# The halves of the second head added by GpSimd, in a new order of VectorE and TensorE, in an attention and feed-forward block

## The chip, the cores and the metric

The kernel runs on one core of a Trainium2 chip. The metric is the device time of one execution in microseconds (us); the median of several executions stands for a kernel.

## The reference

A batch of 64 sequences of 128 rows of width 256 passes a gated cross-attention and a gated feed-forward part. Only the first is touched here.

```python
qh, kh, vh = split_heads(layernorm(x) @ Wq), split_heads(ctx @ Wk), split_heads(ctx @ Wv)   # 16 heads of 64
dots = where(mask or causal, -max, qh @ kh.T * 64 ** -0.5)
x = x + tanh(g_xattn) * (merge_heads(softmax(dots) @ vh) @ Wo + bo)
x = x + tanh(g_ffn) * ffn(layernorm(x))            # quantised activations and weights
```

## The kernel before

Every engine has a program of its own, written out in order by hand, and they meet only at semaphores. The attention runs over 16 groups (`g`) of four sequences, and in each group over 8 steps (`c`) of two heads; `u = 8 g + c` numbers the 128 units. Each engine runs `step(g, c)` for all units through `drive`. `parts` says what a step holds: `new` is the projection of unit `u`, `soft` the softmax of unit `u - 1`, `old` the product with the values of unit `u - 3`; the product with Wo is that of unit `u - 4`.

A unit goes through the engines so. PE makes q and k in two PSUM banks used in turn (`proj`), and a quarter of the values for the group (`jobs` lists them; two banks, so each job waits until the job two places before it has been copied out). ACT copies q and k to SBUF. PE makes the scores of both heads. For each head VectorE (DVE) adds the mask (L635) and takes the maximum (L637), ACT takes four exponentials with their sums (L474), DVE scales the sums by 1/32768 and takes reciprocals (L623, L625), GpSimd (POOL) normalises the probabilities (L423), ACT makes their fp16 high part (L482), POOL the fp16 low part (L428), and a DMA issued by SP turns both parts (L362). DVE adds the two turned halves of each head (`join_prob`, L617), and PE multiplies them with the values (`times_v`, L882). ACT and DVE split that product into `o_hi` (L527) and `o_lo` (L674), which PE multiplies with Wo (`out_product`, L909).

The order in a step is, on PE: q, Wo product of `u - 4`, k, values, `times_v` of `u - 3`, scores of `u`. On DVE: both maxima of `u - 1`, both joins of `u - 3`, reciprocals of the first head, value copies (steps 0 to 2), reciprocals of the second head, then `o_lo` of `u - 3`, whose product is made in this same step, and last the work of the step: row statistics of the next group (step 1), moments (L580 to L588, step 2), statistics and moments of the second layernorm (step 4), its four normalisations (L748, step 5), the maximum (L753) and the four normalisations of the next group's rows (L602, step 6). The mask (step 0) and the residual (L735, step 3) stand earlier. In step 7 PE also turns the next group's rows and context (L853, four jobs `t`), ACT and DVE split each (L467, L610). POOL adds the bias to the residual's rows in step 5 (L439), and takes two powers a group (L415, L419).

The last group is followed by a drain, in which both joins are DVE's.

## Time and profile before

| | us |
|---|---|
| median of 3 runs | 1814.12 (1812.88 to 1816.78) |
| the profiled execution, its own time | 1819.5 |
| its span, first to last instruction | 1817.7 |
| PE, DVE, ACT, POOL busy | 1588.7, 1492.1, 1259.1, 778.9 |
| attention, first q copy to last masked scores | 16.6 to 1231 |
| mean granted TensorE clock | 0.968 |

Busy time is that of all instructions of an engine that overlap nothing of their own; matmuls are pipelined, so a row of one matmul is longer than the time until the next starts. The stages after the attention have the same code in both kernels.

### The profile page before, as it was taken

The page shows a single profiled execution, that of the slowest core. Times are in us where ns is not written, and L with a number is a line of the kernel's source. Part 1 is how long each engine was busy: PE and PEld are TensorE (multiplying, and loading weights), DVE is VectorE, ACT ScalarE, POOL GpSimd, SP SyncE. Part 2 cuts the span into 40 slices and gives each one's busy share as a digit, 9 for nine tenths or more (in the row PEclk, how much of TensorE's full clock was granted, in tenths as well). Part 3 has the DMA queues.
Part 4 walks back from the last instruction along what each step waited for, and adds up shares of the span by engine and source line. Part 5 has one row for each costly group of instructions (what it writes and reads, how often), then busy time and mean ns, then how long its engine had stood idle before and what let it go on. Part 6 is the DMA issues. An engine that isn't in the chain of part 4 may idle for free. (4 is left out here: it accounts for less than half of the span.)

```text
span 1817.7 us, 38253 instructions
## 1 busy us (share of the span) xinstructions
PE 1588.7 (87%) x12684; PEld 1285.3 (71%) x12684; DVE 1492.1 (82%) x2624; ACT 1259.1 (69%) x3238; POOL 778.9 (43%) x622
## 2 busy tenths in 40 slices
PE   7798888988889889898898988887998999895998
PEld 5676776767767677676676766666776777674887
DVE  6787878878788788787887878876888899898997
ACT  5576776766767666676666666665765899896665
POOL 3445545555455454454545545451000666560000
PEclk9899999999999999999999999989999899897999
DMA  5434434434344343344433533243996788474664
GB/s 168 110 83 106 88 88 92 102 86 92 82 92 105 88 98 82 81 107 92 92 82 81 117 82 92 54 87 113 341 327 224 264 279 302 149 289 174 196 208 150
DMA packets 351460, 252.22 MB, mean 139 GB/s; under 512 B 287792, under 2 KB 325808, under 8 KB 348464
## 3 DMA queue, kind: packets, MB, share of 16 engines
q1 hardware_dynamic: 351408, 251.58, 49.1%
q8 instruction: 26, 0.43, 0.1%
q14 instruction: 26, 0.21, 0.0%
HBM read 105.25 MB, written 76.02 MB: 100 GB/s over the span
## 5 line engine op out<-in xcount | busy, mean ns | idle before, releaser
L423 POOL TENSOR_TENSOR prob<-prob,rsums 128x512 f32<-128x512 f32 x256 | 265.5, 1040 | 560.1 <-DVE rsums L625 560.1
L474 ACT ACTIVATE prob<-masked,neg_max 128x128 f32<-128x128 f32 x1024 | 396.5, 389 | 154.5 <-DVE neg_max L637 153.2
L428 POOL TENSOR_TENSOR prob_parts<-prob,prob_parts 128x512 f16<-128x512 f32 x254 | 295.1, 1180 | 3.2 <-ACT prob_parts L482 1.5
L882 PE MATMUL pv<-probT,v_sb 128*64 128x128 f32 x2048 | 154.7, 283 | 112.3 <-DVE probT L617 89.6
L882 PEld LDWEIGHTS pv<-probT,v_sb 128*64 128x64 f32 x2048 | 111.2, 137 | 170.4 <-DVE probT L617 109.5
L482 ACT ACTIVATE prob_parts<-prob 128x512 f16<-128x512 f32 x254 | 160.1, 630 | 68.0 <-POOL prob L423 66.3
L674 DVE TENSOR_TENSOR o_lo<-pv,o_hi 128x512 fp32r<-128x512 f32 x125 | 86.4, 691 | 132.5 <-ACT o_hi L527 132.2
L474 ACT ACTIVATION_READ_ACCUMULATOR prob<-masked,neg_max 128x1 f32 x1024 | 192.6, 188 | 0.0
L637 DVE TENSOR_REDUCE neg_max<-masked 128x4 f32<-128x512 f32 x254 | 174.3, 686 | 8.8
L617 DVE TENSOR_TENSOR probT<-turn 128x512 f32<-128x512 f16 x254 | 172.4, 719 | 3.4 <-DVE mask_add L647 3.4
L635 DVE TENSOR_TENSOR masked<-score,mask_add 128x512 f32<-128x512 f32 x254 | 173.1, 682 | 1.6
L909 PE MATMUL y<-wo_hi,o_hi 128*128 128x256 f32 x508 | 151.5, 298 | 4.4 <-DVE o_lo L674 1.5
L501 ACT ACTIVATE qT<-proj 128x512 f32<-128x512 f32 x128 | 76.8, 600 | 101.1 <-PE proj L826 100.3
L909 PE MATMUL y<-wo_lo,o_hi 128*128 128x256 f32 x508 | 146.6, 289 | 0.0
L909 PE MATMUL y<-wo_hi,o_lo 128*128 128x256 f32 x508 | 146.5, 288 | 0.0
L2090 PE MATMUL y<-wd_both,h_hi 128*128 128x512 f32 x384 | 138.1, 404 | 4.8 <-ACT h_lo L1989 4.8
L1021 PE MATMUL pair<-xThi,wup_hi 128*128 128x512 f32 x312 | 125.2, 401 | 13.6 <-PEq L1381 5.8
L1660 POOL TENSOR_SCALAR xThi<-n_x 128x1024 fp32r<-128x1024 int16 x15 | 44.3, 2953 | 201.2 <-DMA n_x<-n_x_d 166.8
L896 PE MATMUL score<-kT,qT 64*64 64x128 f32 (+1 forms) x4096 | 119.2, 256 | 5.9 <-ACT kT L489 3.9
L1021 PE MATMUL pair<-xThi,wup_lo 128*128 128x512 f32 x312 | 123.7, 396 | 0.0
L1021 PE MATMUL pair<-xTlo,wup_hi 128*128 128x512 f32 x312 | 123.5, 396 | 0.0
L896 PEld LDWEIGHTS score<-kT,qT 64*64 64x64 f32 x4096 | 99.3, 137 | 29.2 <-issue 29.2
(252 smaller groups left out, 4404.0 us busy)
## 6 DMA issues: line engine op xcount, KB each, us to landing
gate<-gate_d SPq DMA_DIRECT2D x30, 768.0 KB, 4.3
n_x<-n_x_d SPq DMA_DIRECT2D x25, 512.0 KB, 5.0
gate_d<-stage SPq DMA_DIRECT2D x8, 1536.0 KB, 5.5
n_u_d<-w_raw SPq DMA_DIRECT2D x16, 768.0 KB, 4.0
stage<-n_u_d SPq DMA_DIRECT2D x16, 768.0 KB, 5.9
gate_d<-gate SPq DMA_DIRECT2D x7, 1536.0 KB, 5.5
x_in<-in_x SPq DMA_DIRECT2D x16, 512.0 KB, 4.2
ctx_in<-in_ctx SPq DMA_DIRECT2D x16, 512.0 KB, 5.1
```

What stands on the lines that cost most here:

```text
L423: gp.tensor_tensor(prob[:, h], prob[:, h], rsums[:, h, :].rearrange("p (b o) -> p b o", o=1).broadcast_to([P, NB, P]), ALU.mult).then_inc( ...
L428: gp.tensor_tensor(prob_parts[:, h, 1], prob[:, h].rearrange("p b k -> p (b k)"), prob_parts[:, h, 0], ALU.subtract).then_inc(prob_low, 1)
L474: nc.scalar.activation(prob[:, h, b, :], masked[:, h, b, :], ACT.Exp, bias=neg_max[:, h, b:b + 1], accum_out=psums[:, h, b:b + 1]).then_in ...
L482: nc.scalar.activation(prob_parts[:, h, 0], prob[:, h].rearrange("p b k -> p (b k)"), ACT.Copy).then_inc(prob_high, 1)
L617: nc.vector.tensor_tensor(probT[:, h], turn[:, slot, h, 0:NB], turn[:, slot, h, NB:2 * NB], ALU.add).then_inc(probT_copied[h], 1)
L635: nc.vector.tensor_tensor(masked[:, h], score[h][:], mask_add[:], ALU.add).then_inc(masked_done, 1)
L637: nc.vector.tensor_reduce(neg_max[:, h, :], masked[:, h], X, ALU.max, negate=True).then_inc(max_done, 1)
L882: last = nc.tensor.matmul(pv[h * HD:(h + 1) * HD, b, :], v_sb[:, b, c * P + h * HD:c * P + (h + 1) * HD], probT[:, h, b, :], start=True, s ...
L896: last = nc.tensor.matmul(score[h][half * HALF:(half + 1) * HALF, b, 0:keys], qT[rows[h], at:at + HALF], kT[rows[h], b * P:b * P + keys], ...
L909: last = nc.tensor.matmul(y[:, e, :], o[s][:, e * P:(e + 1) * P], w[m][:, c * D:(c + 1) * D], start=(c == 0 and j == 0 and e % 2 == 0), st ...
L1021: last = nc.tensor.matmul(bank, stat(s, k), mov(m, k), start=(j == 0), stop=(j == len(passes) - 1))
L2090: nc.tensor.matmul(y[b][:, e], h_hi[:, h, cols], wd[:, :, at:at + D], start=(h == 0 and j == 0), stop=(h == 1 and j == HJ - 1), skip_group ...
```

## The change

The adding of the second head's turned halves moves from DVE to POOL (`join_second`), where it stands first in the step. The scaling of the sums moves from DVE to POOL too, as a product of reciprocal and constant on 128x4 elements before each normalising. On DVE a step now runs: maximum of the first head, `o_lo` of `u - 4` (one step later than before), join of the first head, maximum of the second head, reciprocals, a first part of the step's own work, reciprocals of the second head, value copies, and the rest of that work. PE makes k before the Wo product and not behind it; in step 7 the turnings stand elsewhere. ACT copies k between the exponentials of the two heads in every step. POOL's bias addition moves from step 5 to 6.

```diff
     for c in range(NC):
-        jobs += [(c, "q", 0)]
-        if c == NC - 1:
-            jobs += [(c, "t", n) for n in range(KC)]
-        jobs += [(c, "k", 0)]
+        jobs += [(c, "q", 0), (c, "k", 0)]
         jobs += [(c, "v", n) for n in V_AT[c]]
-    jobs += [(NC - 1, "t", n) for n in range(KC, 2 * KC)]
+    jobs += [(NC - 1, "t", n) for n in range(2 * KC)]
...
             def normalise_prob(u, h):
                 gp.wait_ge(recip_done, 2 * u + h + 1)
-                gp.tensor_tensor(prob[:, h], prob[:, h], rsums[:, h, :].rearrange("p (b o) -> p b o", o=1).broadcast_to([P, NB, P]),
+                gp.tensor_tensor(scaled[:, h], rsums[:, h], pscale[:], ALU.mult).then_inc(sum_scaled, 1)
+                gp.wait_ge(sum_scaled, 2 * u + h + 1)
+                gp.tensor_tensor(prob[:, h], prob[:, h], scaled[:, h, :].rearrange("p (b o) -> p b o", o=1).broadcast_to([P, NB, P]),
                                  ALU.mult).then_inc(normed, 1)
...
+            def join_second(u, slot, times):
+                gp.wait_ge(prob_turned[1][slot], 16 * times)
+                wait(gp, pv_done, u)
+                gp.tensor_tensor(probT[:, 1], turn[:, slot, 1, 0:NB], turn[:, slot, 1, NB:2 * NB],
+                                 ALU.add).then_inc(probT_copied[1], 1)
             def step(g, c):
                 u, new, soft, old, more = parts(g, c)
+                if old:
+                    join_second(u - 3, (c + 1) % 2, NC // 2 * g + (c - 1) // 2)
                 if c == 3 and new and more:
                     make_rstd(g + 1)
                 if c == 5 and new:
                     if not (isinstance(g, int) and g == 0):
                         make_rstd2(g - 1)
+                if c == 6 and new:
                     gp.wait_ge(xres_loaded, 16 * (g + 1))
                     gp.tensor_tensor(xres[:], xres[:], bo_g[:].rearrange("p (o n) -> p o n", o=1).broadcast_to([P, NB, D]),
                                      ALU.add).then_inc(xres_ready, 1)
...
-                if nxt:
-                    for i, n in ts[:KC]:
-                        high(g, i, n)
                 if soft:
                     exps(u - 1, 0)
-                if new and k_first:
+                if nxt:
+                    high(g, *ts[0])
+                if new:
                     copy_k(g, c, u)
                 if nxt:
-                    high(g, *ts[KC])
+                    high(g, *ts[1])
                 if soft:
                     exps(u - 1, 1)
-                if new and not k_first:
-                    copy_k(g, c, u)
                 if nxt:
-                    high(g, *ts[KC + 1])
+                    high(g, *ts[2])
...
+                if nxt:
+                    high(g, *ts[3])
...
             def reciprocals(u, h):
                 dve.wait_ge(exp_done, NB * (2 * u + h + 1))
                 wait(dve, normed, 2 * u + h - 1)
-                nc.vector.tensor_scalar(psums[:, h, :], psums[:, h, :], 1.0 / PSCALE, None, ALU.mult).then_inc(sum_scaled, 1)
-                dve.wait_ge(sum_scaled, 2 * u + h + 1)
                 nc.vector.reciprocal(rsums[:, h, :], psums[:, h, :]).then_inc(recip_done, 1)
+            def maxima(u, h):
+                n = 2 * u + h + 1
+                dve.wait_ge(scored, n)
+                wait(dve, exp_done, NB * (n - 2))
+                nc.vector.tensor_tensor(masked[:, h], score[h][:], mask_add[:], ALU.add).then_inc(masked_done, 1)
+                dve.wait_ge(masked_done, n)
+                nc.vector.tensor_reduce(neg_max[:, h, :], masked[:, h], X, ALU.max, negate=True).then_inc(max_done, 1)
+            def attended_low(u):
+                dve.wait_ge(out_high, u + 1)
+                wait(dve, wo_done, u)
+                nc.vector.tensor_tensor(o_lo[:], hand.banks[1][:], o_hi[:].bitcast(F32), ALU.subtract).then_inc(out_split, 1)
...
                 if soft:
-                    for h in range(2):
...
-                        if nxt:
-                            low(g, *jobs_of(c, "t")[h], 2 * KC * (g + 1) + h)
-                if c == 0 and new:
...
+                    maxima(u - 1, 0)
+                if oldest:
+                    attended_low(u - 4)
                 if old:
-                    for h in range(2):
-                        join_prob(u - 3, h, (c + 1) % 2, NC // 2 * g + (c - 1) // 2)
+                    join_prob(u - 3, 0, (c + 1) % 2, NC // 2 * g + (c - 1) // 2)
                 if soft:
+                    maxima(u - 1, 1)
                     reciprocals(u - 1, 0)
-                if new and c < 3:
...
+                if c == 0:
+                    make_mask(g)
+                if c == 1 and more:
+                    layernorm_stats(g + 1)
+                if c == 2 and more:
+                    layernorm_moments(g + 1)
+                if c == 3 and after_first:
+                    residual(g)
+                if c == 4 and after_first:
+                    second_stats(g - 1)
+                if c == 5 and after_first:
+                    second_norm(g - 1, 0, NB // 2)
+                if c == 6 and after_first and more:
+                    second_max(g - 1)
                 if nxt:
-                    low(g, *jobs_of(c, "t")[KC], 2 * KC * (g + 1) + KC)
+                    for n in range(2):
+                        low(g, *ts[n], 2 * KC * (g + 1) + n)
                 if soft:
                     reciprocals(u - 1, 1)
-                if c == 3 and not (isinstance(g, int) and g == 0):
-                    residual(g)
+                if c < 3:
+                    values(g, c)
+                if c == 4 and after_first:
+                    second_moments(g - 1)
+                if c == 5 and after_first:
+                    second_norm(g - 1, NB // 2, NB)
+                if c == 6 and more:
+                    normalise(g + 1)
                 if nxt:
-                    low(g, *jobs_of(c, "t")[KC + 1], 2 * KC * (g + 1) + KC + 1)
-                if old:
...
-                    nc.vector.tensor_tensor(o_lo[:], hand.banks[1][:], o_hi[:].bitcast(F32), ALU.subtract).then_inc(out_split, 1)
+                    for n in range(2, 4):
+                        low(g, *ts[n], 2 * KC * (g + 1) + n)
...
                         work(n)
-                after_first = new and not (isinstance(g, int) and g == 0)
-                if c == 1 and new and more:
...
-                if c == 6 and new and more:
-                    normalise(g + 1)
...
+            def second_moments(g):
                 moments(stats2, mean2, vare2, stats2_done, MOMENTS * g + NB, var2_ready)
...
-            def second_norm(g):
+            def second_norm(g, first, end):
                 dve.wait_ge(rstd2_ready, g + 1)
                 wait(dve, xn2_stored, 16 * g)
-                for b in range(NB):
+                for b in range(first, end):
                     nc.vector.tensor_scalar(xn2[:, b, :], x1[:, b, :], mean2[:, b:b + 1], rstd2[:, b:b + 1],
...
+            maxima(U - 1, 0)
+            attended_low(U - 4)
             for h in range(2):
                 join_prob(U - 3, h, 1, U // 2 - 1)
+            maxima(U - 1, 1)
             reciprocals(U - 1, 0)
             reciprocals(U - 1, 1)
             attended_low(U - 3)
...
                 src = (x_in, ctx_in)[n // KC]
                 for e in range(NB):
+                    if then is not None and e == NB - 1:
+                        scores_free(*then)
                     last = nc.tensor.transpose(proj[b][:, e * P:(e + 1) * P], src[:, e, (n % KC) * P:(n % KC + 1) * P], ident[:])
                 last.then_inc(projected[b], 1)
...
+                if first or second:
+                    pe.wait_ge(w_ready, 2 if first else 5)
+                if new:
+                    weights_left(g, c, jobs_of(c, "k")[0][0], 1)
                 if nxt:
                     transpose_in(g, *ts[0])
                 if oldest:
...
                     out_product(u - 4, (c - 4) % NC)
                 if nxt:
                     transpose_in(g, *ts[1])
-                if first or second:
-                    pe.wait_ge(w_ready, 2 if first else 5)
-                if new:
-                    weights_left(g, c, jobs_of(c, "k")[0][0], 1)
-                if nxt:
-                    transpose_in(g, *ts[2])
                 if first or fourth:
                     pe.wait_ge(w_ready, 3 if first else 6)
                 if new:
                     for i, n in jobs_of(c, "v"):
                         value(g, i, n)
                 if nxt:
-                    transpose_in(g, *ts[3])
+                    transpose_in(g, *ts[2])
                 if old:
-                    times_v(u - 3, co, (g, c, u) if new else None)
+                    times_v(u - 3, co, (g, c, u) if new and not nxt else None)
+                if nxt:
+                    transpose_in(g, *ts[3], (g, c, u))
                 if new:
-                    if not old:
+                    if not (nxt or old):
                         scores_free(g, c, u)
                     scores(g, c, u)
```

## Rows read from the trace of the kernel before

**Rows 1.** Timeline of ACT, the q copies of step 0 of groups 1 and 15.

```profile
98.17 0.60 ACT L501 ACTIVATE qT<-proj 128x512 f32<-128x512 f32 x1
...
1148.79 0.60 ACT L501 ACTIVATE qT<-proj 128x512 f32<-128x512 f32 x1
```

**Rows 2.** Windows, steps 0 to 7 of group 9, from q copy to q copy; columns: window, length, then busy of each engine.

```profile
698.52:707.90 9.38, 9.37 (x87) 7.83 (x88) 8.15 (x17) 6.22 (x21) 5.05 (x6) 1.00 0.63 168
707.90:715.49 7.59, 7.59 (x80) 6.31 (x80) 5.77 (x15) 6.02 (x22) 4.34 (x5) 1.00 0.39 78
715.49:723.89 8.40, 7.88 (x80) 6.32 (x80) 7.24 (x16) 6.03 (x21) 4.56 (x5) 1.00 0.33 62
723.89:733.56 9.67, 7.89 (x81) 6.33 (x80) 8.90 (x20) 6.39 (x22) 5.44 (x6) 1.00 0.28 54
733.56:741.15 7.59, 7.59 (x80) 6.31 (x80) 5.52 (x13) 6.40 (x22) 4.32 (x5) 1.00 0.79 207
741.15:751.21 10.06, 7.83 (x78) 5.96 (x77) 7.35 (x22) 6.39 (x23) 7.32 (x7) 1.00 0.27 52
751.21:761.43 10.22, 8.04 (x78) 6.16 (x78) 8.12 (x16) 6.38 (x22) 4.58 (x5) 1.00 0.40 103
761.43:774.35 12.92, 10.19 (x88) 8.34 (x88) 9.75 (x21) 7.94 (x25) 3.42 (x4) 0.87 0.21 41
```

**Rows 3.** Timeline of PE, step 1 of group 9: first matmuls of q, Wo product, k, and the rest.

```profile
706.12 0.50 PE L826 MATMUL proj<-tx_hi,wq_hi 128*128 128x512 f32 x1
...
707.61 0.28 PE L909 MATMUL y<-wo_hi,o_hi 128*128 128x256 f32 x1
...
709.02 0.40 PE L826 MATMUL proj<-tc_hi,wk_hi 128*128 128x512 f32 x1
...
711.86 1.09 PE L882 MATMUL pv<-probT,v_sb 128*64 128x128 f32 x16
...
713.71 0.50 PE L826 MATMUL proj<-tx_hi,wq_hi 128*128 128x512 f32 x1
```

**Rows 4.** Waits, 400 to 1200 us: engine, line, releaser, total, times, longest.

```profile
PE pv L882 <- DVE probT L617: 55.2, 31, 3.1
```

**Rows 5.** Timeline of DVE, end of step 4 and start of step 5 of group 9.

```profile
740.43 1.39 DVE L741 BATCH_NORM_STATS2 stats<-x 128x6 f32<-128x256 f32 x4
...
742.77 0.69 DVE L635 TENSOR_TENSOR masked<-score,mask_add 128x512 f32<-128x512 f32 x1
...
745.42 1.87 DVE L617 TENSOR_TENSOR probT<-turn 128x512 f32<-128x512 f16 x2
```

**Rows 6.** Timeline of ACT, step 1 of group 9: q copy, k copy behind eight exponentials.

```profile
707.90 0.60 ACT L501 ACTIVATE qT<-proj 128x512 f32<-128x512 f32 x1 [0.76 <-PE proj L826]
...
711.48 0.57 ACT L489 ACTIVATE kT<-proj 128x512 f32<-128x512 f32 x1
```

**Rows 7.** Timeline of DVE: both joins in step 1, then one sum of the moments in step 2.

```profile
709.36 1.28 DVE L617 TENSOR_TENSOR probT<-turn 128x512 f32<-128x512 f16 x2
...
723.38 1.14 DVE L582 TENSOR_TENSOR v_sum<-stats 128x4 f32<-128x4 f32 x1
```

**Rows 8.** Timeline of POOL, beside the moments of step 2 and the joins of step 5.

```profile
722.19 2.31 POOL L428 TENSOR_TENSOR prob_parts<-prob,prob_parts 128x512 f16<-128x512 f32 x2
...
743.77 2.37 POOL L439 TENSOR_TENSOR xres<-xres,bo_g 128x1024 f32<-128x1024 f32 x1
```

**Rows 9.** Groups of POOL by line, whole span: busy, mean ns, idle before.

```profile
L423 POOL TENSOR_TENSOR prob<-prob,rsums 128x512 f32<-128x512 f32 x256 | 265.5, 1040 | 560.1 <-DVE rsums L625 560.1
...
L415 POOL TENSOR_TENSOR rstd<-vare,mhalf 128x4 f32<-128x4 f32 x16 | 16.3, 1020 | 16.2 <-DVE vare L588 16.2
...
L450 POOL TENSOR_SCALAR tg_small<-tg 128x1 f32<-128x1 f32 x1 | 0.2, 225 | 0.0
```

**Rows 10.** Groups of DVE by line, 400 to 1200 us.

```profile
L623 DVE TENSOR_SCALAR psums<-psums 128x4 f32<-128x4 f32 x170 | 49.4, 291 | 24.4 <-ACT prob L474 24.4
...
L748 DVE TENSOR_SCALAR xn<-x,mean,rstd 128x256 f32<-128x256 f32 x40 | 22.4, 617 | 0.0
```

More of the change, by code:

```diff
@@ L627, in step, with values @@
+            def values(g, c):
+                for i, n in jobs_of(c, "v"):
+                    b, before = nth(g, i)
+                    dve.wait_ge(projected[b], before + 1)
+                    nc.vector.tensor_copy(v_sb[:, n % NB, 0:VH], proj[b][:]).then_inc(copied[b], 1)
             def step(g, c):
                 u, new, soft, old, more = parts(g, c)
+                oldest = not isinstance(g, int) or u >= 4
                 nxt = c == NC - 1 and new and more
+                ts = jobs_of(c, "t")
+                after_first = not (isinstance(g, int) and g == 0)
@@ L767, in _ @@
             drive(dve, step)
-            def attended_low(u):
-                dve.wait_ge(out_high, u + 1)
-                dve.wait_ge(wo_done, u)
-                nc.vector.tensor_tensor(o_lo[:], hand.banks[1][:], o_hi[:].bitcast(F32), ALU.subtract).then_inc(out_split, 1)
             def ffn_low_part(n):
```

63 lines of the change are left out of this document (18 added, 45 removed).

## Prediction

> **What bounds the kernel now.** I read the page first, for the share of each engine, and then only the attention, since the later stages have the same code. The q copies give its beat: from group 1 to group 15 there are 14 groups in 1148.79 - 98.17 us, 75.04 each [rows 1]. Cut at the q copies, the windows show where a group's time lies: steps 1 and 4 take 7.59, the others up to 12.9 [rows 2]. In the two short steps PE is busy without a gap, so 7.59 is PE's own time for a step, and the timeline of one shows its parts: q 1.49, Wo product 1.41, k and values 2.84 together, values' product and scores 1.85 [rows 3]. Step 0 has a second quarter of the values (1.42 more, 9.0). Step 7 has none, but four turnings: four f32 matmuls of 128 columns each; the 16 of the values' product, which run in pairs, take 1.09, so one turning is about 0.52, and the step 7.59 - 1.42 + 2.1 = 8.3. A group in which PE never waits would take 9.0 + 6 x 7.59 + 8.3 = 62.8. It takes 12.2 more.
>
> What PE waits for is the join: 31 waits of 55.2 us in total between 400 and 1200 us [rows 4]. The timeline of DVE around step 5 shows why. The own work of step 4 (statistics from 740.43) stands ahead of the maxima of the next step, which begin at 742.77, and the two joins follow at 745.42 [rows 5]. DVE's cycle is thus: values' product ends, ACT makes `o_hi`, DVE makes `o_lo`, its own work, both maxima (2.65), both joins, and only then PE may multiply again. A step with much own work lengthens PE's step by what is over PE's slack. DVE is not full: 60.8 of 75.8 in this group [rows 2]. POOL is busy 39.0 of them.
>
> **The change part by part.** (1) DVE loses one join a step, 1.28 / 2 = 0.64 [rows 7], and two scalings, 0.29 each [rows 10]: 1.2 x 8 = 9.8 a group. It is left with 51 of PE's 62.8. (2) The order: I follow one step from the start of q, at 0. Scores are there at about 0.2. DVE: first maximum to 1.5, `o_lo` (as long as one mask addition, 0.66) to 2.2, join to 2.85, second maximum to 4.2, reciprocals, first own part from 4.4. ACT copies q at 1.8 [rows 3, 6] and, since eight exponentials take 3.09 less the copy's 0.5, say 1.55 a head, has the first head done at 3.8, k copied at 4.4, the second head done at 5.95. The second reciprocals come at 6.1. PE wants `o_lo` at 1.49 + 1.41 = 2.9, the joins and k at about 5.75, and is through at 7.59. So in a bare step nothing waits, and own work of 1.7 us between the two reciprocals lies beside the exponentials, where it costs nothing; with no such cover it would cost what it costs now. That takes away the 12.2 but for what follows. The wait for the k copy at the values' product goes too, because k is made 1.41 sooner and copied before the second head.
>
> What is late next? `o_lo` is now made in the very step that uses it, with 0.7 us of slack. Whatever DVE still does when the scores are there, beyond that, stops PE. Behind the second reciprocals, at 6.3, there are 1.5 us left to the next scores: enough for values, not always for moments (step 4) and four normalisations (step 6).
>
> (3) The price of POOL. Its join is not in the trace; a product over the same 128x512 takes 1.04 [rows 9] and the low parts 2.31 for two [rows 8]; I take 1.17. Its scaling on 128x4 is bounded by 0.23 (a small one-input instruction) and 1.02 (a power on 128x4) [rows 9]. A power is not a product, so I take 0.3 with its wait. A step costs POOL 1.17 + 2 x 0.3 + 2 x 1.04 + 2.31 = 6.2, and a group with two powers and the bias addition (2.37 [rows 8]) 49.6 + 4.4 = 54, under 62.8. The order within POOL is good: its second low part ends about 2.2 us into the next step, the join to 3.4, and PE wants it at 5.75. SP's queue keeps its order; the turning of a head has three steps until its join, against a landing of a few microseconds, so I cost it at nothing; the low parts and the next high part are half a step apart.
>
> (4) Collisions. Two DVE instructions show that a POOL instruction can hold them up: the 128x4 sum at 723.38 took 1.14 [rows 7], to the end of the second low part, which ran from about 723.35 to 724.50 [rows 8]; and the joins at 745.42 took 1.87 and not 1.28 [rows 5, 7], while the bias addition ran until 746.14 [rows 8]. The scaling's mean of 0.29 and 0.617 for 256 columns of the second normalisations [rows 10] fit: instructions that read two things from SBUF wait. Additions with a PSUM input, as the maxima's, show none. The Trainium skill, SBUF — State Buffer, section "SBUF: two separate sides", says the same: one shared pair, an exclusive lock for the whole instruction. By that rule the collisions are whole POOL instructions and not a shared pace, and the trace agrees (the sum ends with the low part, to 0.02 us).
>
> POOL is now busy nearly without a break from the second reciprocals (6.2) to 3.4 in the next step. So the parts that DVE does behind the second reciprocals run into it. Step 4: seven small instructions, of which two or three are held for 1.04 to 1.17: they end 2.2 late, less 0.7 of slack, 1.6 us of wait (between 0 and 2.7). Step 5: two normalisations there, 0.3 (0 to 1.5). Step 6: four of them, and the bias addition has just pushed POOL back; they end 1.6 to 5.2 into step 7, which needs them for its first turning and `o_lo`; with the serial chain of turnings, copies and low parts in step 7 I take 2.5 (1.2 to 4.8). Step 7 itself: the fourth low part waits for ACT, which has four more copies than usual, and ends about 1.5 into step 0: 0.8. The other five steps together 0.3. The sum is 5.5 of the 12.2 back: a group of 68.3, or 6.8 less than now, 14 x 6.8 = 95. In groups 0 and 15, which have loads and weight work of their own, I take 5 each, as the same order holds but DVE has more own work (nothing to 10 each). The drain keeps its instructions. Together 105.
>
> The same skill, GPSIMD Engine Reference, section "Engine selection", speaks against moving an addition: elementwise work belongs on VectorE, where two-input work is about twice as fast. The rows agree, 0.64 against 1.04 to 1.17. It would make the join dearer by 0.5 a unit, which would tell only if POOL were the bound.
>
> The sum is made against the profiled execution: 1819.5, of which the span is 1817.7 and 1.8 lies around it. It gives 1714.5. That execution is 5.4 above the median of the runs, 1814.12, more than their highest; I apply the same saving to the median: 1709.
>
> **Rivals.** A: the collisions are nearly harmless (the lower ends: 0, 0, 1.2, 0.5). A group of 64.5, 147 saved, with 12 for groups 0 and 15: 1655. For it: DVE has 51 us of work, and a short instruction may slip in between two of POOL. B: they are at their upper ends (2.7, 1.5, 4.8, with 1 each for step 7 and the rest): 73.8 and 17 saved, 1790; halfway between it and mine 71, 57 + 5 saved, 1752. For it: POOL's chain of product, two low parts and join is 4.4 us without a gap, and it is the very stretch in which DVE's late parts stand; step 7's stop also fell with the clock, 0.87 in its window [rows 2], which a longer stop brings back. C, the other side: POOL becomes the bound. If the 128x4 product costs 1.02 as the power does, with 0.1 for its wait, a step is 7.8, a group 62 + 4.4, plus the joins that hold it (8 x 0.64) and six more held instructions of 0.35 and moments, some 4: 76, or 1 x 14 slower, 1828. It decides from about 1.0 us for that product on; below 0.6 POOL has slack again. Against it: 0.23 for the other small instruction. D: no change within 0.2%, because the beat is set by something that I don't see, 1814; the two steps at exactly 7.59 with PE full speak against it.
>
> **How the numbers follow.** Mine (1680 to 1740) 0.5; A 0.17; B with its half way 0.23; D 0.03; C 0.07. The predicted time is 1709. Faster by over 0.2% (3.6 us, about what a measurement of this kernel can tell from no change) are mine, A and nearly all of B: 0.89; same 0.03, slower 0.08. The range for 8 in 10 leaves out half of A's lower side and the upper end of B with C: 1655 to 1775.
>
> **What the profile after would show.** Right: q copies 68 apart a group; steps 0 to 3 within 0.3 of PE's own time; no wait of the values' product for a join of DVE, but waits of the Wo product for `o_lo` and of the first turning for DVE in steps 5 and 7; POOL's 128x4 product near 0.2 and its join near 1.17; POOL busy about 140 + 60 us more; single small DVE instructions of about 1 us ending with one of POOL. Wrong: waits for POOL's join at the values' product (C); steps 5 and 7 at 7.6 and 8.3 (A); waits of ACT for a turned part before the high parts, which I cost at nothing.

## The result, and the profile after

The changed kernel takes 1677.05 us (median of 4 runs, 1674.65 to 1681.05) against 1815.45 (1812.88 to 1817.66) for the kernel before in the same session: a ratio of 0.924 (95% interval 0.9217 to 0.9264), 138 us less. The forecast was 1709 in a range of 1655 to 1775. The profiled execution took 1674.65, its span is 1672.8, which is 144.9 less than the 1817.7 of before.

Each engine's busy time over the span, from the page of the changed kernel:

```profile
PE 1558.6 (93%) x12684; PEld 1270.2 (76%) x12684; DVE 1376.2 (82%) x2243; ACT 1254.1 (75%) x3238; POOL 1022.8 (61%) x1004
```

DVE has 116 us less work than before (1492.1), POOL 244 more (778.9), while PE and ACT have the same work. The mean granted clock is 0.977 (0.968). The timeline of ACT gives the beat of the groups, again from the q copies of groups 1 and 15, beside [rows 1]:

```profile
92.91 0.60 ACT L509 ACTIVATE qT<-proj 128x512 f32<-128x512 f32 x1 [0.56 <-PE proj L840]
...
1012.55 0.60 ACT L509 ACTIVATE qT<-proj 128x512 f32<-128x512 f32 x1 [0.47 <-PE proj L840]
```

That is 65.69 a group where it was 75.04: 14 x 9.35 = 131 of the 145 us. Group 0 takes 76.7 and not 81.6, group 15 to its last q copy 67.2 and not 72.9, another 10.6. Some 3 us lie elsewhere. The windows of group 9, steps 0 to 7, beside [rows 2]:

```profile
618.47:628.13 9.66, 9.38 (x86) 7.45 (x86) 7.38 (x15) 6.11 (x21) 6.91 (x9) 1.00 0.62 165
628.13:635.75 7.62, 7.62 (x80) 6.33 (x79) 6.59 (x14) 5.99 (x21) 4.94 (x7) 1.00 0.37 74
...
651.00:658.62 7.62, 7.62 (x80) 6.33 (x79) 7.06 (x19) 6.37 (x22) 6.43 (x8) 1.00 0.79 206
658.62:666.56 7.94, 7.89 (x80) 6.25 (x79) 6.42 (x14) 6.57 (x22) 6.80 (x8) 1.00 0.34 66
666.56:675.16 8.60, 8.38 (x82) 6.64 (x81) 8.01 (x14) 6.28 (x22) 8.44 (x9) 1.00 0.47 122
675.16:684.16 9.00, 8.07 (x87) 6.45 (x86) 5.59 (x11) 7.71 (x27) 6.94 (x9) 1.00 0.30 58
```

Steps 1 to 4 (2 and 3 are left out, 7.62 and 7.63) are PE's own time, with PE busy throughout. What is left over it is 0.32 in step 5, 0.98 in step 6, and about 0.7 each in steps 0 and 7, where PE's own time, 9.0 and 8.3, is the prediction's reckoning and not a measurement. Step 7 was 12.92 and at a clock of 0.87; it is 9.00 at full clock.

The waits of the changed kernel, 400 to 1000 us (engine, line, releaser; total, times, longest):

```profile
PEld y L925 <- DVE o_lo L643: 10.7, 18, 0.7
...
PEld proj L840 <- DVE tc_lo L617: 8.5, 18, 0.7
...
PE proj L869 <- ACT kT L498: 3.6, 9, 0.4
...
PE proj L840 <- ACT v_sb L528: 2.1, 9, 0.3
```

The wait of the values' product for a join, 55.2 us in [rows 4], is gone. What remains of PE's waits is short. In PE's own rows it is 4.7 us for the low parts of the turned rows and 2.6 for `o_lo`, both DVE's, and 5.7 for ACT's copies of k and of the values. None is put down to the join that POOL now makes. The two groups of POOL that are new, over the whole span (busy, mean ns, idle before):

```profile
L434 POOL TENSOR_TENSOR probT<-turn 128x512 f32<-128x512 f16 x125 | 177.7, 1421 | 0.0
L420 POOL TENSOR_TENSOR scaled<-rsums,pscale 128x4 f32<-128x4 f32 x256 | 58.8, 230 | 181.7 <-DVE rsums L630 181.4
```

The small product costs 0.23, and the join 1.42 where 1.17 was taken.

The step with the most over PE's own time is step 6. This is its end in group 9, POOL first, then DVE, then ACT:

```profile
669.28 2.38 POOL L448 TENSOR_TENSOR xres<-xres,bo_g 128x1024 f32<-128x1024 f32 x1
```

```profile
671.42 2.08 DVE L609 TENSOR_SCALAR x_in<-x_in,mean,rstd 128x256 f32<-128x256 f32 x4
```

```profile
673.15 0.63 ACT L491 ACTIVATE prob_parts<-prob 128x512 f16<-128x512 f32 x1 [1.85 <-POOL prob L422]
...
675.16 0.60 ACT L509 ACTIVATE qT<-proj 128x512 f32<-128x512 f32 x1
```

The bias addition makes POOL's first product late (it ends at 673.03). ACT waits 1.85 for it, and the copy of the values and that of q stand behind it in ACT's order. PE's k then waits 0.22 for the value copy (at 674.32). The q copy that ends this window is late too, so part of the 0.98 is PE's only in step 7: from q's first matmul to the next, the two steps take 7.64 and 9.95 (664.80, 672.44, 682.39). PE waits 0.41 there for ACT's copy of k (at 678.31) and 0.52 for the low part of the third turning (at 682.39). Between 400 and 1000 us it never waits for `x_in`, although the four normalisations take 2.08.

Now the collisions. DVE at the end of step 4 of group 9:

```profile
655.19 0.18 DVE L630 RECIPROCAL rsums<-psums 128x4 f32<-128x4 f32 x1 [0.42 <-ACT prob L483]
655.30 0.17 DVE L587 TENSOR_TENSOR m_sum<-stats 128x4 f32<-128x4 f32 x1
...
655.73 0.16 DVE L592 TENSOR_TENSOR m_sq<-m_dif 128x4 f32<-128x4 f32 x1
655.80 1.03 DVE L593 TENSOR_SCALAR v_eps<-v_sum 128x4 f32<-128x4 f32 x1
656.86 1.09 DVE L595 SCALAR_TENSOR_TENSOR vare<-m_sq,v_eps 128x4 f32<-128x4 f32 x1
```

and POOL beside it:

```profile
651.41 1.69 POOL L434 TENSOR_TENSOR probT<-turn 128x512 f32<-128x512 f16 x1
...
655.45 0.23 POOL L420 TENSOR_TENSOR scaled<-rsums,pscale 128x4 f32<-128x4 f32 x1 [0.57 <-DVE rsums L630]
655.76 1.04 POOL L422 TENSOR_TENSOR prob<-prob,scaled 128x512 f32<-128x512 f32 x1
656.76 2.29 POOL L427 TENSOR_TENSOR prob_parts<-prob,prob_parts 128x512 f16<-128x512 f32 x2
```

Of seven instructions on 128x4, five take 0.16 and two take 1.03 and 1.09. `v_eps` starts with POOL's product and ends as that ends (655.80 + 1.03 = 656.83, against 656.76 to 656.80). `vare` is let in there and ends with the first low part. The other five start from 655.30 to 655.73, before POOL's product (655.76): a window of some 0.4 us behind the reciprocals, open because POOL first makes its own small product.

### The profile page after: what moved, and what is told of

Its sections match the earlier page's. It is cut to its first block and busy times, and to the rows that moved or that the text cites. A ratio compares the mean times of both kernels' runs of the same rounds, so it can differ in the third digit from the quotient of the medians.

```text
span 1672.8 us, 38339 instructions
## 1 busy us (share of the span) xinstructions
PE 1558.6 (93%) x12684; PEld 1270.2 (76%) x12684; DVE 1376.2 (82%) x2243; ACT 1254.1 (75%) x3238; POOL 1022.8 (61%) x1004
## 5 line engine op out<-in xcount | busy, mean ns | idle before, releaser
L427 POOL TENSOR_TENSOR prob_parts<-prob,prob_parts 128x512 f16<-128x512 f32 x254 | 299.3, 1197 | 4.2 <-ACT prob_parts L491 2.4
L422 POOL TENSOR_TENSOR prob<-prob,scaled 128x512 f32<-128x512 f32 x256 | 269.8, 1054 | 20.0
L434 POOL TENSOR_TENSOR probT<-turn 128x512 f32<-128x512 f16 x125 | 177.7, 1421 | 0.0
L420 POOL TENSOR_TENSOR scaled<-rsums,pscale 128x4 f32<-128x4 f32 x256 | 58.8, 230 | 181.7 <-DVE rsums L630 181.4
L898 PE MATMUL pv<-probT,v_sb 128*64 128x128 f32 x2048 | 141.6, 281 | 3.7 <-DVE probT L624 2.8
L925 PE MATMUL y<-wo_lo,o_hi 128*128 128x256 f32 x508 | 144.9, 285 | 0.0
L2106 PE MATMUL y<-wd_both,h_hi 128*128 128x512 f32 x384 | 134.6, 394 | 4.7 <-ACT h_lo L2005 4.7
L925 PEld LDWEIGHTS y<-wo_hi,o_hi 128*128 128x128 f32 x508 | 97.3, 191 | 37.4 <-DVE o_lo L643 34.4
L624 DVE TENSOR_TENSOR probT<-turn 128x512 f32<-128x512 f16 x129 | 123.4, 958 | 0.0
```

The costliest lines, as they stand in the source:

```text
L422: gp.tensor_tensor(prob[:, h], prob[:, h], scaled[:, h, :].rearrange("p (b o) -> p b o", o=1).broadcast_to([P, NB, P]), ALU.mult).then_inc ...
L427: gp.tensor_tensor(prob_parts[:, h, 1], prob[:, h].rearrange("p b k -> p (b k)"), prob_parts[:, h, 0], ALU.subtract).then_inc(prob_low, 1)
L434: gp.tensor_tensor(probT[:, 1], turn[:, slot, 1, 0:NB], turn[:, slot, 1, NB:2 * NB], ALU.add).then_inc(probT_copied[1], 1)
L624: nc.vector.tensor_tensor(probT[:, h], turn[:, slot, h, 0:NB], turn[:, slot, h, NB:2 * NB], ALU.add).then_inc(probT_copied[h], 1)
L898: last = nc.tensor.matmul(pv[h * HD:(h + 1) * HD, b, :], v_sb[:, b, c * P + h * HD:c * P + (h + 1) * HD], probT[:, h, b, :], start=True, s ...
L925: last = nc.tensor.matmul(y[:, e, :], o[s][:, e * P:(e + 1) * P], w[m][:, c * D:(c + 1) * D], start=(c == 0 and j == 0 and e % 2 == 0), st ...
```

## The experiments

Times are medians and the ratios are to the kernel before in the same session, with the 95% interval. "Group" is the mean of the 14 groups, read as above from the q copies. An edit is against the changed kernel unless it says otherwise.

**Both joins on DVE again, in the new order.**

```diff
-                if old:
-                    join_second(u - 3, (c + 1) % 2, NC // 2 * g + (c - 1) // 2)
...
                 if old:
-                    join_prob(u - 3, 0, (c + 1) % 2, NC // 2 * g + (c - 1) // 2)
+                    for h in range(2):
+                        join_prob(u - 3, h, (c + 1) % 2, NC // 2 * g + (c - 1) // 2)
```

> The changed kernel with both joins back on VectorE, one behind the other, and everything else as changed: the new order without the second head's offload. My theory (VectorE is not full; what paid is that its own work and the low part no longer stand between two products with the values): the second join delays the second maximum, and so the second exponentials, by 0.6 us, of which the step has most in hand; a group goes from 65.7 to some 66.3, the kernel to about 1686. Rival (the offloaded join is a real part of the gain): each step is longer by about the join's 0.64 us, a group 70.8, the kernel about 1755.

Measured: 1752.33, 0.966 (0.9644 to 0.9676), a group of 70.75. The steps of group 9 are 9.57, 7.62, 7.62, 7.66, 7.90, 9.19, 10.18, 11.29. In size that is the rival's, but not in its manner: steps 0 to 3 have not grown, so a second join has room on DVE in a bare step. All of it is in steps 4 to 7, and the timeline of DVE in this kernel shows how, at the end of step 6:

```profile
713.26 4.49 DVE L622 TENSOR_TENSOR probT<-turn 128x512 f32<-128x512 f16 x2
```

with POOL beside it:

```profile
714.36 2.84 POOL L446 TENSOR_TENSOR xres<-xres,bo_g 128x1024 f32<-128x1024 f32 x1
```

Two joins of 0.64 each take 4.49. The pair starts beside the low parts and ends 0.55 behind the bias addition (717.20), about the length of one join. So a part of what the joins on DVE cost is time in which POOL holds them; a later run shows how much goes with the bias addition. My figure had left that out.

**The moved work alone, in the order of before.** The second join and the scaling go to POOL as in the change; all else is the kernel before, against which the diff stands. It shows the join alone; the scaling's lines are those of the change.

```diff
                 if old:
-                    for h in range(2):
-                        join_prob(u - 3, h, (c + 1) % 2, NC // 2 * g + (c - 1) // 2)
+                    join_prob(u - 3, 0, (c + 1) % 2, NC // 2 * g + (c - 1) // 2)
...
+                if old:
+                    join_second(u - 3, (c + 1) % 2, NC // 2 * g + (c - 1) // 2)
```

> The kernel before, in its old order, with the second head's join and the scalings of both heads moved to GpSimd: the offload without the order. My theory: VectorE's cycle from one product with the values to the next is shorter by 0.64 us in the five or six steps that are bound by it, a group 71.5, the kernel about 1765. Rival (the offload is what pays): most of the 138 us, about 1690 to 1710. Other rival (in the old order GpSimd's join comes too late or collides): no gain, 1815.

Measured: 1846.0, 1.0181 (1.0163 to 1.0199), a group of 76.79. The sign was wrong. The waits of this kernel, 400 to 1200 us:

```profile
PE pv L893 <- DVE probT L631: 39.9, 30, 2.9
PE pv L893 <- ACT kT L503: 34.3, 40, 1.2
```

The wait for DVE's join fell only from 55.2 [rows 4] to 39.9, and that for k's copy rose (14.5 before). And what DVE does on its own became slower, here the moments of step 2, DVE and then POOL:

```profile
740.67 1.14 DVE L596 TENSOR_TENSOR v_sum<-stats 128x4 f32<-128x4 f32 x1
741.85 1.09 DVE L598 TENSOR_SCALAR mean<-m_sum 128x4 f32<-128x4 f32 x1
```

```profile
739.49 2.29 POOL L433 TENSOR_TENSOR prob_parts<-prob,prob_parts 128x512 f16<-128x512 f32 x2
741.75 1.16 POOL L440 TENSOR_TENSOR probT<-turn 128x512 f32<-128x512 f16 x1
```

POOL's join stands right behind the low parts, and so holds the next of DVE's instructions: `mean` averages 631 ns between 400 and 1200 us where it was 170, a normalisation of `xn` 862 (617, [rows 10]), one of `x_in` 647 (406), all over the same stretch.

**The moved work alone, with k copied between the exponentials in every step.** This takes away the wait for k and asks whether it was the cause. The diff is against the last kernel.

```diff
-                k_first = c in (0, NC - 1)
+                k_first = True
```

> The kernel before in its old order, with join and scalings moved to GpSimd as in the run before on this (1846), and ACT's copy of k between the two heads' exponentials in every step. In that run the product with the values waited less for the join (39.9 against 55.2 us in 800) but more for k's copy (34.3 against 14.5). Theory: the wait for k, which stands behind both maxima and all exponentials, took up what the shorter join gave: with k copied early the gain comes out, a group 73 to 74.5, the kernel about 1795. Rival (the loss is GpSimd's join holding up VectorE's own work, and k only fills in): about 1835 to 1846.

Measured: 1871.36, 1.0306 (1.0281 to 1.0331), a group of 78.55. The wait for k is gone, and the time is still 25 us more:

```profile
PE pv L893 <- DVE probT L631: 61.3, 31, 2.8
...
PE proj L864 <- DVE x_in L616: 44.6, 11, 4.1
```

The wait for k had only filled in ahead of that for DVE. The copy in its new place also makes the second head's sums later: DVE waits 84.5 us for exponentials where it waited 64.5. My expectation fell. The rival had the loss stay with k copied early, but it gave 1835 to 1846, and no run here separates what POOL's join holds up from the rest of the 31 us.

**The Wo product ahead of k again.**

```diff
+                if oldest:
...
+                    out_product(u - 4, (c - 4) % NC)
...
                 if new:
                     weights_left(g, c, jobs_of(c, "k")[0][0], 1)
...
-                if oldest:
...
-                    out_product(u - 4, (c - 4) % NC)
```

> The changed kernel with PE's Wo product again ahead of k, VectorE's new order kept. By my step table PE then wants the low part at 1.5 us of a step, and VectorE has it at 2.25: 0.7 us of wait in all 8 steps, not given back, so a group of 71.5 and the kernel about 1770. Rival (the low part is ready earlier than I worked out, or the delay is absorbed): 1677 to 1685.

Measured: 1895.89, 1.0454 (1.0435 to 1.0472), a group of 79.54. Every bare step has about the wait that the reckoning in the prediction gives (0.7 of slack less 1.41), as PE's timeline shows:

```profile
767.39 0.39 PE L925 MATMUL y<-wo_hi,o_hi 128*128 128x256 f32 x1 [0.64 <-DVE o_lo L643]
```

Steps 1 to 4 take 8.52 to 8.58, 0.9 more, together 3.6 of the 12.7 that group 9 has grown by (the row ahead of a wait is longer than PE's pace, so a row's wait is less than what the step grows by). The rest is in steps 5, 7 and 0 (10.01, 14.62, 11.03), where PE waits 2.13, 2.70 and 1.76 for `o_lo`. That fits a slack of nothing, at which whatever makes DVE late goes to PE in full. I had counted the first part only.

**All own work of DVE behind the second reciprocals and value copies.**

```diff
                 if c < 3:
                     values(g, c)
+                if c == 0:
+                    make_mask(g)
+                if c == 1 and more:
+                    layernorm_stats(g + 1)
...
```

> The changed kernel with all own work of VectorE's step (mask, statistics, moments of the first layernorm, residual, first two normalisations, maximum) behind the second reciprocals and the value copies, none between the two reciprocals. My theory: the stretch between the reciprocals is free time beside the exponentials, and behind them only 1.5 us are left and GpSimd is in the way: waits of PE for the low part in steps 2, 4, 5 and 6, a group of about 70, the kernel about 1740. Rival (VectorE has slack enough, the place doesn't matter): 1677 to 1685.

Measured: 1870.9, 1.0309 (1.0292 to 1.0326), a group of 79.1. The direction was right; the size is three times what I gave, 194 us and not 63. The worst is step 3 with 13.26. Ahead of it, DVE has the moments of step 2 beside POOL's whole chain:

```profile
751.86 0.89 DVE L587 TENSOR_TENSOR m_sum<-stats 128x4 f32<-128x4 f32 x1
752.67 0.15 DVE L588 TENSOR_TENSOR m_dif<-stats 128x4 f32<-128x4 f32 x1
752.74 1.14 DVE L589 TENSOR_TENSOR v_sum<-stats 128x4 f32<-128x4 f32 x1
753.91 1.08 DVE L591 TENSOR_SCALAR mean<-m_sum 128x4 f32<-128x4 f32 x1
...
754.98 1.12 DVE L593 TENSOR_SCALAR v_eps<-v_sum 128x4 f32<-128x4 f32 x1
```

Seven instructions on 128x4, 0.86 us when nothing holds them (below), take 4.4. PE then waits 3.85 for `o_lo` (at 758.42). The mean clock is 0.947.

**The bias addition in step 7, between POOL's two products.**

```diff
-                if c == 6 and new:
-                    gp.wait_ge(xres_loaded, 16 * (g + 1))
...
                         normalise_prob(u - 1, h)
+                        if h == 0 and c == 7 and new:
+                            gp.wait_ge(xres_loaded, 16 * (g + 1))
...
```

> The changed kernel with GpSimd's bias addition (2.4 us) moved from step 6, ahead of both products, to step 7, between the two. My theory: the 1.0 us that step 6 and the 0.5 us that step 7 take over PE's own time come from the addition, which makes the first product, ACT's high part and the value copy behind it late; a group goes from 65.7 to some 64.4, the kernel to about 1658. Rival (VectorE's four normalisations are what is late): 1677, as they stay where they are. Other rival (in step 7 it makes the second product late and comes back in step 0): 1677 or more.

Measured: 1686.76, 0.9289 (0.9273 to 0.9305), a group of 66.18, 0.5 more than the changed kernel. Step 6 fell to 7.63 as forecast, but step 7 rose to 10.01 and step 5 to 8.46. The four normalisations at the end of step 6, in this kernel:

```profile
675.74 2.92 DVE L609 TENSOR_SCALAR x_in<-x_in,mean,rstd 128x256 f32<-128x256 f32 x4
```

They took 2.08 in the changed kernel (671.42 to 673.50). There the bias addition had pushed POOL back, and its first product ended at 673.03, with 0.3 until the second. Now the product (676.26 to 677.34) is followed by two low parts without a gap. In step 7 PE now waits 0.42 for `o_lo`, which it did not in the changed kernel. So the addition was what made step 6 long, as in my theory, but moving it made a collision elsewhere. Step 5's 0.5 more goes with a wait of 0.57 for `o_lo`; why it grew was not followed up.

**Normalisations between the reciprocals in step 6, the maximum behind them,** on top of the last edit. The maximum reads one tensor and nothing else.

```diff
-                if c == 6 and after_first and more:
-                    second_max(g - 1)
+                if c == 6 and more:
+                    normalise(g + 1)
...
-                if c == 6 and more:
-                    normalise(g + 1)
+                if c == 6 and after_first and more:
+                    second_max(g - 1)
```

> The changed kernel with the bias addition in step 7, as in the run before, and in step 6 the four normalisations between the reciprocals and the maximum (which reads one SBUF operand) behind them. With the addition alone moved, step 6 lost its 1.0 us, but the normalisations met the second product and the low parts, took 2.9 us and not 2.1, and step 7 was 1.0 longer. My theory: between the reciprocals they meet one product at most, and the maximum behind them is not held: a group of 65.0, the kernel about 1668. Rival (the four are held as long there, and the second reciprocals come late instead): 1680 or more.

Measured: 1664.78, 0.9164 (0.9148 to 0.918), a group of 65.02. Step 7 is 9.01 again and step 6 stays at 7.63. The maximum, now beside POOL's chain, takes 1.18 us in all ten groups between 400 and 1000 us, and it took 1.19 in the changed kernel, inside the bias addition (669.61 to 670.80): POOL doesn't hold it.

**The moments of step 4 between the reciprocals too,** on top of that.

```diff
                 if c == 4 and after_first:
                     second_stats(g - 1)
+                    second_moments(g - 1)
...
-                if c == 4 and after_first:
-                    second_moments(g - 1)
```

> The kernel of the run with the bias addition in step 7 and the normalisations of step 6 between the reciprocals (1665), and in step 4 the seven moments' instructions ahead of the second reciprocals instead of behind them. Behind them the last two are held by GpSimd's second product and first low part, about 1 us each, and step 5 is 8.25 and not 7.62. My theory: ahead of them GpSimd's first product is over and nothing holds them; the second reciprocals are 0.7 us late, which GpSimd makes good in the next step; step 5 at 7.65 to 7.8, a group of 64.5, the kernel about 1657. Rival (the late reciprocals only move the whole chain and step 5 meets it with the second product for the values): 1665 or more.

Measured: 1657.21 (1655.95 to 1658.63), 0.9129 (0.9116 to 0.9141), a group of 64.44. The moments of step 4 run ahead of the second reciprocals, all seven at their own length; of these the first and last:

```profile
641.97 0.17 DVE L587 TENSOR_TENSOR m_sum<-stats 128x4 f32<-128x4 f32 x1
...
642.67 0.16 DVE L595 SCALAR_TENSOR_TENSOR vare<-m_sq,v_eps 128x4 f32<-128x4 f32 x1
```

POOL is between its two products there (none from 642.04 to 643.10). The moments of step 2 stand between the reciprocals as well, and there `vare` is still held by the first product, 0.88 at 626.34, at no cost: steps 1 to 6 are now 7.62 or 7.63. This kernel beats both: 1.2% less than the changed one (0.9129 / 0.924). In group 9 PE has two waits left, 0.28 for `o_lo` in step 0 (at 607.29) and 0.33 for the low part of the third turning (at 668.28).

**In step 7, the third high part of the turned rows ahead of the second exponentials.**

```diff
                 if nxt:
                     high(g, *ts[1])
-                if soft:
-                    exps(u - 1, 1)
                 if nxt:
                     high(g, *ts[2])
                 if soft:
+                    exps(u - 1, 1)
+                if soft:
                     high_prob(u - 1, 0, c % 2, NC // 2 * g + c // 2)
```

> The changed kernel with ACT's copy of the third turning (step 7) ahead of the second head's exponentials. My theory: the 0.5 us that q waits in step 0 for the low part of that turning go, and nothing else becomes late: a group 65.2, the kernel about 1669. Rival (the exponentials, the second product and the low parts are 0.5 us later, and the wait for the Wo product's low part in step 0 grows by as much): 1677.

Measured: 1680.09, 0.925 (0.9233 to 0.9267), a group of 65.91: no gain. The wait that should have gone is still there: the q of step 0 waits 0.63 where it waited 0.52.

**POOL's join made twice,** the first time into a tile that nobody reads; this is added work, and nothing is left out.

```diff
+                gp.tensor_tensor(spare[:], turn[:, slot, 1, 0:NB], turn[:, slot, 1, NB:2 * NB], ALU.add)
                 gp.tensor_tensor(probT[:, 1], turn[:, slot, 1, 0:NB], turn[:, slot, 1, NB:2 * NB],
                                  ALU.add).then_inc(probT_copied[1], 1)
```

> The changed kernel with GpSimd's addition of the halves made twice in every step, first into a spare tile: GpSimd has 1.2 us more a step. My theory: GpSimd is not the bound, in steps 0 to 2 and 4 the second addition fits ahead of the first product, and only steps 3, 5, 6 and 7, which have the powers and the bias addition, get longer: a group 67 to 69, the kernel about 1710. Rival (GpSimd with 54 us a group is as good as the bound): 8 x 1.2 = 9.4 a group, the kernel about 1825.

Measured: 1726.45, 0.9514 (0.9486 to 0.9541), a group of 68.88; steps 9.66, 7.62, 7.63, 8.39, 7.91, 8.49, 10.20, 9.00. In steps 0 to 2 another 1.2 us on POOL costs nothing, so POOL is not the bound there. It costs in steps 3 to 6, which have powers, the bias addition or late parts of DVE: 3.2 a group for 8 x 1.2 of work. In step 6 PE waits 1.36 for ACT's copy of the values (0.22 in the changed kernel), as the first product is later still.

**Both joins on DVE, and the bias addition in step 7.** This tests whether the first experiment's loss comes from the joins being held by the bias addition.

The edit is that of the bias addition, on top of the first experiment (the lines taken out of step 6 are left out):

```diff
                         normalise_prob(u - 1, h)
+                        if h == 0 and c == 7 and new:
+                            gp.wait_ge(xres_loaded, 16 * (g + 1))
...
```

> Both joins on VectorE, as in the run before on this, and the bias addition in step 7. There the joins of step 6 took 4.5 us instead of 1.3, held to the end of the bias addition. Theory of the collisions (what the offload saves is not the join's 0.64 us but that VectorE stands behind GpSimd's chains): step 6 and 7 lose most of their surplus of 3.9 us over the changed kernel, a group 68.5, the kernel about 1715. Rival (it is VectorE's load): 1750, unchanged.

Measured: 1717.76, 0.9464 (0.9442 to 0.9486), a group of 68.29. Of the 75 us that the joins on DVE cost, 35 go with the place of one POOL instruction, though in the changed kernel the same move costs 9 (0.9289 against 0.924). Step 6 falls from 10.18 to 7.98. The other 40 stay. They are in steps 5 (9.19 as before) and 7 (10.87) above all, where PE waits 1.63 and 1.19 for `o_lo`. A second join of 0.64 makes DVE that much later in the step, and its last two moments are held for 1.03 and 1.09 as in the changed kernel; how much of the 40 is length and how much is holding was not separated.

**The scaling back on DVE, the join on POOL.**

```diff
-                gp.tensor_tensor(scaled[:, h], rsums[:, h], pscale[:], ALU.mult).then_inc(sum_scaled, 1)
-                gp.wait_ge(sum_scaled, 2 * u + h + 1)
...
+                nc.vector.tensor_scalar(psums[:, h, :], psums[:, h, :], 1.0 / PSCALE, None, ALU.mult).then_inc(sum_scaled, 1)
+                dve.wait_ge(sum_scaled, 2 * u + h + 1)
                 nc.vector.reciprocal(rsums[:, h, :], psums[:, h, :]).then_inc(recip_done, 1)
```

> The changed kernel with the scaling of the sums back on VectorE, ahead of the reciprocals; the join stays on GpSimd. My theory: 0.16 us of VectorE for 0.28 us of GpSimd's chain, both with room in most steps, so 1670 to 1685, no difference beyond 0.5%. Rival (VectorE's scalings are held behind GpSimd's product, as some were in the kernel before, 0.7 us each): a group 67 or more, the kernel about 1700.

Measured: 1748.69, 0.9639 (0.9618 to 0.9661), a group of 70.5. About half a microsecond a step on DVE, in a kernel whose bare steps have room for it, costs 72 us. The end of step 4, DVE:

```profile
697.16 0.18 DVE L630 RECIPROCAL rsums<-psums 128x4 f32<-128x4 f32 x1
...
697.62 0.90 DVE L589 TENSOR_SCALAR mean<-m_sum 128x4 f32<-128x4 f32 x1
...
698.51 1.14 DVE L591 TENSOR_SCALAR v_eps<-v_sum 128x4 f32<-128x4 f32 x1
699.68 1.08 DVE L593 SCALAR_TENSOR_TENSOR vare<-m_sq,v_eps 128x4 f32<-128x4 f32 x1
```

and POOL:

```profile
697.42 1.07 POOL L420 TENSOR_TENSOR prob<-prob,rsums 128x512 f32<-128x512 f32 x1 [0.77 <-DVE rsums L630]
```

POOL's product now starts 0.26 after the start of the reciprocals and not 0.57, and three moments are held, not two. It is the same with the normalisations: `x_in` averages 1004 ns against 579, `xn` 737. (Means over 400 to 1200 us; `xn` took 401 in the changed kernel.) So the small product on POOL bought a window. It is not the only thing that it bought, for the scaling itself is held as well, once in every group, to the end of the bias addition, DVE and then POOL:

```profile
713.68 1.05 DVE L628 TENSOR_SCALAR psums<-psums 128x4 f32<-128x4 f32 x1
```

```profile
711.86 2.84 POOL L446 TENSOR_TENSOR xres<-xres,bo_g 128x1024 f32<-128x1024 f32 x1
```

In 9 of 16 groups this takes 2.17, in 7 it takes 1.05; the mean over all scalings, 265 ns, hides it. PE waits for `o_lo` 1.95 in step 5 and 1.19 in step 7 of group 9. The 72 us were not divided between the two.

## Why the prediction was right, and where its sizes were off

**The bound and the order: right.** The own work of DVE in front of the joins was what PE waited for: put behind the second reciprocals it costs 194 us. The order with the scaling on POOL, but not the join, gives 62 of the 138 us (first experiment), and bare steps run at PE's own 7.62. The slack of 0.7 at `o_lo` was worked out well: take away the 1.41 of the Wo product and PE waits 0.64 in each bare step. The copy of k at the values' product went as forecast.

**The fall of DVE's load (9.8 a group): too large, and wrong as a reason.** In group 9 DVE's busy time fell from 60.8 to 53.4, that is by 7.4, as instructions that POOL holds count as busy (the first join now averages 0.96 and not 0.72). Join and scaling on POOL in the old order made the kernel 31 us slower, while in the new order the join's move is worth 75 and the scaling's 72. Their worth is not simply in what DVE no longer does, as bare steps take either on DVE without a loss. The parts need each other.

**POOL's prices: nearly right.** The small product 0.23 and not 0.3, the join 1.42 and not 1.17. Alone it takes 1.17; the rest is its wait for DVE's join, which reads SBUF at the same time (1.69 at 651.41). The lock holds in both directions, which the forecast did not price. POOL was busy 54.5 of group 9, forecast 54. Rival C fell with the 0.23, and the doubled join shows room left in the bare steps.

**Collisions: the mechanism right, the size too large, and one path missed.** This is the step that was off: 5.5 a group was taken, 2.9 is measured over PE's 62.8. Moments and second normalisations together: 0.3 and not 1.9, because two moments are held but the other five pass ahead of POOL's product, and the slack takes up most of the two. For the four normalisations of step 6 and the chain behind them 2.5 was taken. They took 2.08, held by one product of POOL, the next mask addition follows at 673.43, and PE waits neither for `x_in` nor, in step 7, for `o_lo`. What steps 6 and 7 have over PE's time, 1.0 + 0.7, came in good part by a path that the forecast had no term for. The bias addition delays POOL's first product, ACT waits for that, and from 673.15 to its copy of k at 677.67 it has no gap left, so that its copies of the values and of k are late for PE. The run with the addition in step 7 shows it for step 6, which falls to 7.63. That this stood in the place of a term that did not come was luck. The 0.8 put down for the low parts at the end of step 7 is a wait of 0.52 of the next q, and step 0 has 0.65, with 0.28 of wait for `o_lo`. So the group, 65.69, lies between mine (68.3) and that of rival A (64.5). Between the profiled executions the forecast of 1714.5 missed 1674.65 by 39.9, of which 14 x 2.6 = 36 are this term.

**The rule for what is held: too narrow.** The prediction had instructions that read two things from SBUF wait, and counted the scaling among them, which reads one tensor and a constant. The traces show that it is held all the same (1.05 at 713.68, to within 0.03 of the end of the bias addition). Of the signs that the prediction named, three did not come: step 0 has 0.65 over PE's time and not 0.3, the first turning didn't wait for DVE, and the Wo product waited for `o_lo` in steps 0 and 5 and not in step 7. Two slips move nothing: 17 saved gives rival B 1797 and not 1790, and 75.0 less 68.3 is 6.7 and not 6.8.

The Trainium skill, SBUF — State Buffer, section "SBUF: two separate sides", names an exclusive lock for a whole instruction, and the traces agree: instructions on 128x4 last up to 1.14 us and end with POOL's (656.83 against 656.80 for the one of 1.03). The Trainium skill, GPSIMD Engine Reference, section "Engine selection", keeps elementwise work on VectorE. Here the old order agrees (31 us more with join and scaling on POOL) and the new one does not (75 less for the join alone). The join's own length on POOL is nearly the same in both (1.17 and 1.42), so it is not what decides.

**Groups 0 and 15:** 4.9 and 5.8 against 5 and 5.

**What stays open.** In the best version steps 0 and 7 are 0.6 and 0.7 over the reckoned 9.0 and 8.3. PE's two waits there, 0.28 and 0.33, are a part of it; the rest may be PE's own time, which was not measured without waits. The new order with neither piece of work moved, and the old one with only one of them, were not run, so what the order alone is worth, and how the 31 us are shared between join and scaling, is open.

## What to carry to other kernels

When VectorE and GpSimd both read tensors in SBUF, cost a move between them by which instructions will run side by side and which of them somebody waits for, not by their durations. Put VectorE's small dependent instructions on SBUF where GpSimd is between two of its own, or where nobody waits for them (here between two reciprocals, while ScalarE works), and beside GpSimd's chain what the trace shows is not held (here reciprocals, a maximum and additions with a PSUM input). Follow a late GpSimd instruction through ScalarE too. A late consumer needs slack for the holds ahead of it (about 1.1 us each here), or they go to TensorE.

## What the runs showed of the hardware that was not expected

- A chain of small instructions goes at GpSimd's pace. Each end of a GpSimd instruction let in the one that was held and, at most, one that followed with nothing to wait for: with all own work late, `m_sum`, `v_sum`, `mean` and `v_eps` take 0.89 to 1.14 each, `m_dif` and `m_sq` 0.15 (`m_sq` at 754.91), though these read SBUF in the same way.
- `TENSOR_SCALAR` on 128x4 and 128x256 with its scalars in SBUF is held as two-input ones are (`mean` 1.08, `x_in` up to 2.92 for four). So is a scaling of one 128x4 tensor by a constant: in the kernel before 63 of the 256 take 0.45 to 0.70 us and the others 0.15 to 0.17, and a long one ends with POOL's product (49.90 + 0.69 against 49.53 + 1.04). A reciprocal (178 ns at most) and a maximum over one tensor (1.18 to 1.22 for 128x1024) are not.
- After a stop of PE the granted clock fell, in the second experiment. PE had been idle for 2.3 of the 4.2 us from 745.0 to 749.2 there; windows of 1 us of that kernel:

```profile
749.00:750.00 1.00, 1.00 (x30) 0.83 (x32) 0.63 (x2) 1.00 (x3) 1.00 (x2) 0.71 0.00 0
750.00:751.00 1.00, 1.00 (x17) 0.84 (x10) 0.89 (x2) 0.45 (x1) 1.00 (x2) 0.50 0.00 0
...
752.00:753.00 1.00, 1.00 (x4) 0.81 (x3) 0.96 (x3) 0.00 (x0) 0.94 (x1) 0.59 1.10 208
```

  0.50 is 1.2 GHz (the window left out has 0.50 too). Over these four windows that is (0.29 + 0.50 + 0.50 + 0.41) = 1.7 us of PE's work at full speed that was lost behind the stop, an estimate; in the changed kernel, whose longest waits of PE are 0.7, group 9 has 1.00 in all eight windows.
